# A two-layer state-space block: the last 64 channels in halves on 128 partitions, paired projections, step lengths with B and C, decays one unit ahead

## The reference

```
x = x + L0(group_norm(x))     # 32 groups of 6 channels
x = x + L1(group_norm(x))
```

```
dt  = softplus(dt + dt_bias);  cs = cumsum(dt * A) within the chunk
att[i,j,h] = (C_i . B_j) * exp(cs_i - cs_j) * dt_j      for j <= i
y = att @ x + C . state * exp(cs);   y = y + D * x
out = (layer_norm(y) * z) @ out_proj.T
```

```
delta = softplus(delta + dt_bias)
h[d,n] = exp(delta_d * A[d,n]) * h[d,n] + delta_d * x_d * B_n;   y_d = sum_n h[d,n] * C_n
out = (y + D * x) @ W_out.T + b_out
```

## Time and profile before

| | |
|---|---|
| median of three runs | 3382.27 us (3380.13 to 3385.87) |
| the profiled execution | 3382.05 us, span 3380.3 us |
| PE | 2844.2 us busy, 84% |
| PEld (weight loads) | 1502.5 us, 44% |
| DVE | 2711.6 us, 80% |
| ACT | 1929.9 us, 57% |
| POOL | 1593.6 us, 47% |
| granted PE clock, mean | 0.92 |
| DMA | mean 86 GB/s; a shifted copy lands 2.9 us after its issue (median) |

### The profile page before, as it was taken

How to read it: one execution, slowest core, us unless ns; L and a number is a source line. 1 busy time by engine, 2 the same in 40 slices (tenths; PEclk the granted TensorE clock), 3 DMA queues, 4 the chain that set the end, 5 groups by cost and what they waited for, 6 DMA issues and landing times. The chain is left out here.

```text
span 3380.3 us, 62242 instructions
## 1 busy us (share of the span) xinstructions
PE 2844.2 (84%) x20640; PEld 1502.5 (44%) x20640; DVE 2711.6 (80%) x4364; ACT 1929.9 (57%) x4507; POOL 1593.6 (47%) x1235
## 2 busy tenths in 40 slices
PE   3788888988888898888888888898888988888865
PEld 2554536353453634445354453544445354443510
DVE  1357979789697978979689797978969798797997
ACT  1637475564657547475664746547475664746542
POOL 2114545454454545545355444545545455554555
PEclk8989999899999989999899989989999999989976
DMA  2132141422314142241423215142241424214131
GB/s 52 25 99 70 60 139 49 131 73 86 97 54 137 54 129 78 68 123 54 120 73 106 82 50 140 51 141 73 74 109 54 119 73 123 79 58 128 42 113 59
DMA packets 104163, 290.97 MB, mean 86 GB/s; under 512 B 25373, under 2 KB 27020, under 8 KB 103820
## 3 DMA queue, kind: packets, MB, share of 16 engines
q1 hardware_dynamic: 103820, 286.71, 28.5%
HBM read 181.84 MB, written 39.85 MB: 66 GB/s over the span
## 5 line engine op out<-in xcount | busy, mean ns | idle before, releaser
L754 POOL TENSOR_TENSOR hc<-hst,bcrep 128x512 f32<-128x512 f32 x768 | 1202.0, 1565 | 1155.8 <-DVE hst L1249 1127.6
L1298 PE MATMUL bank<-hc,sel 128*32 128x512 f32 x1536 | 435.4, 650 | 113.3 <-POOL hc L754 109.5
L1236 DVE TENSOR_TENSOR wr<-durep,bcrep 128x512 f32<-128x512 f32 x768 | 520.1, 677 | 2.9 <-DMA bcrep<-bc_rows 2.9
L1249 DVE TENSOR_TENSOR_SCAN hst<-dec,wr 128x512 f32<-128x512 f32 x256 | 396.0, 1547 | 99.0 <-ACT carry L991 71.2
L842 ACT ACTIVATE ssd<-bank,ncs 128x128 f32<-128x128 f32 x1536 | 438.3, 385 | 48.7 <-PE bank L1298 47.0
L1298 PE MATMUL bank<-xna,wt0a 128*128 128x128 f32 (+3 forms) x1088 | 303.5, 381 | 46.0 <-DVE xnb L1056 27.6
L1249 DVE TENSOR_TENSOR_SCAN hst<-bank,carry,wr 128x512 f32<-128x512 f32 x240 | 306.4, 1277 | 22.7 <-ACT bank L950 13.3
L950 ACT ACTIVATE bank<-durep,aneg 128x512 f32<-128x512 f32 x368 | 251.3, 687 | 121.0 <-DVE hst L1249 63.3
L1298 PE MATMUL bank<-ssd,wcv 64*32 64x512 f32 (+1 forms) x6144 | 307.6, 543 | 0.0
L950 ACT ACTIVATE dec<-durep,aneg 128x512 f32<-128x512 f32 x400 | 290.3, 731 | 6.4 <-DVE hst L1249 4.7
L1298 PE MATMUL bank<-xnb,wt0b 128*128 128x128 f32 (+3 forms) x1088 | 289.3, 368 | 0.0
(11 more groups left out here) (189 smaller groups left out, 4975.3 us busy)
## 6 DMA issues: line engine op xcount, KB each, us to landing
durep<-scratch SPq DMA_DIRECT2D x192, 512.0 KB, 3.8
bcrep<-bc_rows SPq DMA_DIRECT2D x128, 512.0 KB, 4.9
ssd<-stage SPq DMA_DIRECT2D x384, 140.4 KB, 2.9
ssd<-bcst SPq DMA_DIRECT2D x128, 74.4 KB, 2.7
xa<-in_x_dram SPq DMA_DIRECT2D x16, 512.0 KB, 4.1
...
```

The costliest lines, as they stand in the source:

```text
L754: nc.gpsimd.tensor_tensor(hc[:, i % CRING, :], hst[:, i % HRING, :], bcrep[:, g, 1, :], ALU.mult).then_inc(hc_ready.sem, 1)
L1236: nc.vector.tensor_tensor(wr[:, i % WRING, :], durep[:, j % SLOTS_DU, 1, :], bcrep[:, g, 0, :], ALU.mult).then_inc(w_made.sem, 1)
L1249: nc.vector.tensor_tensor_scan(hst[:, i % HRING, :], decay_of(i), wr[:, i % WRING, :], carry[:, g:g + 1] if hf else 0.0, ALU.mult, ALU.add ...
L1298: return nc.tensor.matmul(out, lhsT, rhs, start=start, stop=stop, skip_group_check=True)
```

## The change

- The last 64 channels lie in tiles of 128 partitions by 512 tokens: tokens 0-511 on partitions 0-63, tokens 512-1023 on 64-127. Loads, stores, statistics and the normalisation follow; the group matrix `gb` is doubled and halved for it. The gate, which needs one half per chunk, has weights with zeros in the other half's rows (`wtz`).
- `fill` and `project` work in pairs: both halves' K=128 matmuls, then both K=64 ones, on rows 0-63 and 64-127 of the array, each into its own bank.
- The step lengths are projected with B and C: 76 columns. VectorE adds the bias while it reads them from the bank, TensorE turns them to tokens with four transposes (`step_lengths`), ScalarE copies them. There are eight fills instead of nine, and B and C have two staging tiles.
- The biases of L1's projections are added by ScalarE as it copies. The projections stand at slots 40 to 43 in the order dA, BC, xA, xdB, each for both halves.
- ScalarE makes decay s+1 in slot s (0 and 1 in slot 0), and the carry right behind it instead of at the slot's end. The first nine units take banks 0, 1 and one SBUF buffer in turn, where the first eight took banks 0 and 1.

```diff
-FILL_AT = (0, 0, 1, 1, 1, 1, 2, 2, 2)
-FILL_COPY_AT = (0, 0, 1, 1, 2, 2, 2, 3, 3)
+FILL_AT = (0, 0, 1, 1, 1, 1, 2, 2)
+FILL_COPY_AT = (0, 0, 1, 1, 2, 2, 3, 3)
-P1_AT = (4, 4, 5, 7, 7, 8, 9, 10)
+P1_AT = (4, 5, 6, 7)
+FRONT_UNITS = 9
 def decay_bank(i):
-    if i < 8 or i >= 38:
+    if i < FRONT_UNITS:
+        return (0, 1, None)[i % 3]
+    if i >= 38:
         return i % 2
     return 6 + i % 2 if 31 <= i < 36 else None
...
@@ scalar: copy_fill
+                m, h = FILL_TILES[k]
+                if m == XM:
+                    nc.scalar.copy(staged(bcst[h], 1)[0:2 * NS, :, :], by_row[0:2 * NS, :, :])
+                    if h == 0:
+                        return
+                    r, other = 17 * PW + 1, bank[FILL_BANKS[(k - 1) % 3]]
+                    nc.scalar.copy(bcst[1][0:2 * NS, 1:W + 1], other[0:2 * NS, HALF - W:HALF]).then_inc(fill_copied.sem, 1)
+                    ins = nc.scalar.copy(bcst[0][0:2 * NS, r:r + W], ps[0:2 * NS, 0:W])
...
@@ scalar: run
-                        decay(b, s, end, first)
+                        for i in (0, 1) if s == 0 else (s + 1,) if s + 1 < UNITS else ():
+                            decay(b, i, end, first)
+                        if 2 <= s < HU + 2:
+                            keep_carry(b, s - 2)
                     if first:
                         first_block(b + 1, s, step, 1 - par, scan, end)
-                        if 2 <= s < HU + 2:
-                            act.wait_ge(scanned.sem, scanned.at(b, s - 1))
-                            nc.scalar.copy(carry[:, s - 2:s - 1], hst[:, (s - 2) % HRING, HALF - 1:HALF]).then_inc(carried.sem, 1)
...
@@ vector
-                nc.vector.bn_aggr(mv[0:CB_, 1, :], st[0:CB_, 1, :, :].rearrange("p a s -> p (a s)")).then_inc(stats_ready.sem, 1)
+                nc.vector.bn_aggr(mv[:, 1, :], st[:, 1, 0, :]).then_inc(stats_ready.sem, 1)
-                if s == 3:
-                    dve.wait_ge(fill_copied.sem, fill_copied.at(n, 7))
-                    nc.vector.tensor_tensor(dtx[:, :, :], dtx[:, :, :], bc(dtb[:, :].unsqueeze(1), [P, NCH, NH]),
-                                            ALU.add).then_inc(dtx_ready.sem, 1)
+                if s == 2:
+                    dve.wait_ge(fill_ps.sem, fill_ps.at(n, 6))
+                    for h in range(2):
+                        nc.vector.tensor_scalar(dtt[(1 - h) * CB_:(1 - h) * CB_ + NH, :], bank[FILL_BANKS[(4 + h) % 3]][2 * NS:2 * NS + NH, :],
+                                                dtb[2 * NS:2 * NS + NH, :], None, ALU.add).then_inc(dtt_ready.sem, 1)
...
@@ tensor: fill
+                ps = [bank[FILL_BANKS[(k + h) % 3]] for h in range(2)]
+                for h in range(2):
+                    if k + h >= 3:
+                        pe.wait_ge(fill_copied.sem, fill_copied.at(n, k + h - 2))
+                    if k + h == 7:
+                        pe.wait_ge(dtt_ready.sem, dtt_ready.at(n, 1))
+                    mm(ps[h][0:w, :], wt0a[:, c0:c0 + w], xna[:, h * HALF:(h + 1) * HALF], True, False)
+                for h in range(2):
+                    rows = slice(h * CB_, (h + 1) * CB_)
+                    mm(ps[h][0:w, :], wt0b[rows, m * P:m * P + w], xnb[rows, :], False, True).then_inc(fill_ps.sem, 1)
+            def step_lengths(n):
+                pe.wait_ge(dtt_ready.sem, dtt_ready.at(n, 2))
+                pe.wait_ge(fill_copied.sem, fill_copied.at(n, 6))
+                for c in range(CPH):
+                    ins = nc.tensor.transpose(bank[B_DT][:, c * P:(c + 1) * P], dtt[:, c * Q:(c + 1) * Q], ident[:, :])
+                ins.then_inc(dt_ps.sem, 1)
...
@@ tensor: gate, project
-                    ins = mm(o, wt0b[:, m * P:(m + 1) * P], xnb[:, t], False, True)
+                    ins = mm(o, wtz[:, c // CPH, m * P:(m + 1) * P], xnb[:, c % CPH * Q:(c % CPH + 1) * Q], False, True)
...
+                for h in range(2):
+                    mm(outs[h], wt1a[:, c0:c0 + w], xna[:, h * HALF:(h + 1) * HALF], True, False)
+                for h in range(2):
+                    rows = slice(h * CB_, (h + 1) * CB_)
+                    mm(outs[h], wt1b[rows, c0:c0 + w], xnb[rows, :], False, True).then_inc(p1_ps.sem, 1)
```

More of the change, by code:

```diff
@@ L94 @@
 MID = 1
-P1_TILES = (("dA", 0), ("BC", 0), ("xA", 0), ("xdB", 0), ("xdB", 1), ("dA", 1), ("xA", 1), ("BC", 1))
-K_BC, K_XA, K_MID, K_D2, K_X2 = 2, 3, 5, 6, 7
+P1_PIECES = ("dA", "BC", "xA", "xdB")
+P1_TILES = [(what, h) for what in P1_PIECES for h in range(2)]
+BIAS = {"dA": 0, "xdB": 1, "xA": 2, "BC": 3}
+K_D2, K_BC, K_XA, K_X2, K_MID = 2, 3, 5, 6, 8
 K_ALL = len(P1_TILES)
@@ L280, in build @@
         x1a = [sb(f"x1a{p}", [P, L]) for p in range(2)]
-        x1b = [sb(f"x1b{p}", [CB_, L]) for p in range(2)]
+        x1b = [sb(f"x1b{p}", [P, HALF]) for p in range(2)]
         xcm = sb("xcm", [P, 3, HALF])
@@ L849, in first_block @@
                         copy_fill(n, k)
+                if s == 3:
+                    act.wait_ge(dt_ps.sem, dt_ps.at(n, 1))
+                    by_half = bank[B_DT][:, :].rearrange("p (c h k) -> p h c k", c=CPH, h=2)
+                    for h in range(2):
+                        ins = nc.scalar.copy(dtx[:, h * CPH:(h + 1) * CPH, :], by_half[:, 1 - h, :, 0:NH])
+                    ins.then_inc(dtx_ready.sem, 1)
                 if s == 4:
@@ L1630 @@
 EXP_LN = "natural_log_exp_and_others"
-NLOADS = 76
-PREPS = 12
+NLOADS = 79
+PREPS = 14
 DVE_STEPS = 35
```

236 lines of the change are left out of this document (119 added, 117 removed).

## The result

The changed kernel takes 3360.33 us (median of 4, 3355.22 to 3361.96), the kernel before beside it 3384.07 us (3380.13 to 3385.88): a ratio of 0.9929 with a 95% interval of 0.9912 to 0.9946. It is faster by 24 us. The forecast was 154 us, so 130 us did not come, and the time lies outside the range.

What follows compares the result with a forecast made beforehand. Bounds: TensorE in a pass's front, a multi-engine loop in chunks, VectorE in the tail. 7.9 + 2.2 = 10.1 us per pass, 152 over 15 passes, plus 6, less 2 and 1.7: 154 us saved, 3228 us, range 3178 to 3318.

Steps and rivals of the forecast that it cites:

- Fills: Front of a pass: paired fills with overlapping row halves and no small records save 6.4 us, leaving about 16 us.
- rival 1: Fills: row halves don't overlap or the half clock stays, 3 to 3.4 us a pass, 3278 us; chance 0.13.
- the 0.8 us of waiting: Fills: the sixth waits for the third's copy, behind ScalarE's two decays; 0.8 us more, between 0 and 2.
- The last convolution, for which 6.6 us were forecast: After the fills: TensorE's slot 10 and last convolution start 6.6 us earlier (6.4 passed on, 0.3 lost, 0.5 gained).
- First attention: First attention product: 6.6 us plus about 1.3 from carry copies ahead of the SiLUs, 7.9 us per pass.
- ScalarE's stall on scan 8: Slot 8: ScalarE waits about 2.5 us, scan 10 about 4; priced at 0, 2.5 a pass without the convolution's cover.
- Chunks: Chunk steps: the loop stays 10.3 us against a period of 10.37; change 0, bounds -0.2 and +0.5 per chunk.
- Rival 4: Chunks: slower, as ScalarE held behind scans falls behind; 1.5 us per chunk would give 3408 us; chance 0.08.
- Tail: End of a pass: fewer statistics passes and narrower normalisation save VectorE 1.6 us, 2.2 us per pass in all.
- the projections' 4 us of TensorE lie beside VectorE: Tail: the projections' 4 us of TensorE work run beside VectorE, which was taken for the chain.
- Beginning: Start of the kernel: three more loads and their copies ahead of everything cost 2 us.
- Rival 2: Front's gain is used up again; only VectorE's 2.2 us a pass in the tail remain, 3349 us; chance 0.12.

Runs made afterwards that it cites:

- own steps: Changed kernel with ScalarE's decays and carries back in their own steps and in their old buffers: 3341.86 us, 0.9885.
- own_tail: Changed kernel with decays one unit ahead up to unit 30 and in their own steps from unit 31 on: 3359.59 us, 0.9940.
- shifted buffers: Changed kernel with the three SBUF decay buffers shifted by one from unit 9 on, so decay 9 no longer needs scan 8's buffer: 3339.71 us, 0.9886.

## Why the prediction was wrong

- **Fills: right in kind, too large on the mean.** 16.2 us against 16 in the shown pass, overlap as taken, last pair at the full clock: rival 1 is refuted. Part of the agreement is luck: the 0.8 us of waiting did not come, and the half clock at the fills' start, on which the forecast put no change, lasts 4.9 us (1225.83 to 1230.7) instead of about 3.4. On the mean the fills up to the first convolution are 4.8 us shorter (21.2 to 16.4), not 6.4: the forecast was worked out from one pass, one of the six of twelve in which they took 22.3 us or more. That is 1.6 us a pass. They also begin 0.8 us earlier behind the normalisation of xa. The last convolution, for which 6.6 us were forecast, starts 4.8 us earlier. That scan 14 is 6.8 us earlier looks like the 6.6, but it is a different path, the one on which the late carry before scan 12 (3.6 us on the mean) is gone and a new one before scan 10 (3.7) has come.
- **First attention: the step that failed first.** The forecast turned 6.6 into 7.9 and priced ScalarE's stall on scan 8 at 0, because TensorE's last convolution needs neither. The stall was seen (3.67 us, 2.5 said; scan 10 waits 3.71, 4 said), and the last convolution does not need it: without the stall it starts only 0.4 us earlier. But the exponents of chunk 0 need ScalarE; without the stall they start 1.7 us earlier and the first attention product 2.4. In the changed kernel that product is 4.0 us earlier than before instead of 7.9: 1.8 us were missing at the last convolution, 2.1 more behind it. Removing the stall alone gave 20.6 us, own steps 18.5.
- **Chunks: right** up to scan 32 (82.9 us from scan 15, before 83.5). Rival 4 is refuted. But from unit 31 on the ring has two banks, and the decay of step 33 holds chunk 7's normalisation: 1.7 us a pass between scans 32 and 33. The prediction looked at one chunk in the middle and carried it over the ring's change.
- **Tail: -2.2 us forecast, +0.7 measured** (scan 33 to the end, 45.3 against 44.6 us). The saved statistics are real: VectorE's work there went from 41.0 to 39.5 us, the 1.6 us that were forecast. Its waits went from 3.5 to 5.8 us. The step "the projections' 4 us of TensorE lie beside VectorE" is what failed: a pair gives its first half a matmul later, xA stands a step later, xdB stands ahead of the group variance. Reordering gave 39 us.
- **Beginning: 8.2 us against 2.** Four more loads (82 instead of 78) are issued, and the first weight copy starts 3.8 us later (49.58 against 45.80). ScalarE makes 51 copies instead of 40, which takes 4 us more. The largest groups of copies:

```profile
L806 ACT COPY wt1b<-bank 64x64 f32<-64x64 f32 (+2 forms) x12 | 2.6, 213 | 0.2
L806 ACT COPY wt0b<-bank 64x128 f32<-64x128 f32 (+1 forms) x8 | 2.0, 247 | 0.1
L806 ACT COPY wtz<-bank 64x128 f32<-64x128 f32 x6 | 1.5, 258 | 0.1
```

Together: 10.1 forecast, less 3.9 to the first attention product, 1.7 at scan 33 and 2.9 in the tail, and 0.6 more in the chunks, is the 2.2 us a pass that the table has. Rival 2 was the nearest (3349), but it left VectorE's 2.2 us of the tail untouched, and those went too. Of the 130 us that did not come, the stall and the order of the projections account for some 20 and 39 by the runs that took them out, the fills' smaller gain for some 24 (1.6 us in 15 passes, an estimate) and the beginning for 6. Decays in their own steps at the ring's change gave nothing alone (own_tail) and 21 us once the projections were reordered. These do not add up exactly, since one wait often takes another's place. How the loss before scan 15 divides between ScalarE's amount of work and the stall is not settled: with shifted buffers it is still 6.95 us from scan 14 to 15, against 4.72 before.
